# GpSimd splits the row maxima; fp32 exponentials stay in PSUM, with three banks of logits and one of products

## The chip, the core and the metric

The kernel runs on one core of a Trainium2 chip. The metric is device time in microseconds (us) from the start to the end of one execution. Before the change it is 1060.51 us, the median of 3 runs (1059.92 to 1063.94). The engines are TensorE (PE in the profile, with its weight loads as PEld), VectorE (DVE), ScalarE (ACT), GpSimd (POOL) and SyncE (SP), which here only issues DMAs.

## What is computed

A gated cross-attention block followed by a gated feed-forward block with ternary weights, for 8 batches of 224 query rows and 750 context rows of width 512, 16 heads of 32:

```python
q = layer_norm(layernorm(x), gq, betq); c = layer_norm(ctx, gkv, betkv)
Q, K, V = q @ Wq + bq, c @ Wk + bk, c @ Wv + bv          # split into 16 heads
attn = softmax(Q @ K.T * 32**-0.5)                        # 224 x 750 for each head
x = x + tanh(g_xattn) * ((attn @ V) @ Wo + bo)
h = relu(layernorm(x) @ ternary(W1).T + b1)               # 2048 wide
out = x + tanh(g_ffn) * (h @ ternary(W2).T + b2)
```

## The kernel before

Precision comes from pairs of fp16: an operand is kept as a high half and a low half (the fp32 value less the high half), and products of the halves are summed in PSUM.

The work of the batches is a pipeline. `ORDER` lists eleven bodies: OPEN and FIRST (set-up, and the preparation of batch 0), SECOND (attention of batch 0, together with the comparison of the weights that makes them ternary), five INNER bodies, THIRD_LAST, SECOND_LAST and LAST. An INNER body does the attention of one batch, prepares q, k and v of the next (`PREP`), finishes the one before (`FINISH`: normalise, project, feed forward) and normalises the input of the one after the next. Each body has 16 slots, one per head, and `slot_steps` writes the order of the steps in a slot by hand; every engine walks through the same list in order and does its own part of each step. With w0, w1 and w2 for the extra work that `SLOT_WORK` (and `SECOND_WORK`, `SECOND_LAST_WORK`) gives a slot, the order is: score 0, expo 0, w0, expo 1, score 1, w1, expo 2, pv, w2.

- `score` (L437, L776): TensorE makes 128 queries x 750 keys for the head four ahead, in two banks, `ps_score`, which hold one score. VectorE takes the row maximum into `mx` (L779). TensorE's next score waits for that (`max_taken`, L442).
- `split_max` (L782): at the start of every even slot VectorE scales the maxima of two heads by 1/16 and splits them into two fp16 halves, `mhl` (L785, L788). The step `mr` (L518) turns them into rows by four small matmuls, ScalarE copies them into `q_stack`, and the logits of these heads then carry minus the row maximum.
- `expo` (L450, L633, L792): a head has three units of 2 x 125 keys x 224 queries. TensorE writes the logits of a unit into one of two banks, `ps_exp`. ScalarE takes the exponential twice, first in fp32 into `p_full` in SBUF (L642, two buffers), then in fp16 into `ph` (L644). VectorE subtracts: `pl = p_full - ph` (L796). In VectorE's list this stands one unit later than in TensorE's: at expo 0 it does unit 2 of the head before, at expo 1 unit 0, at expo 2 unit 1.
- `pv` (L462): products of `ph` and `pl` with V for the head before, into one of two banks, `ps_pv`; VectorE sums the halves into `o_sum` (`take_o`, L799).
- Fill steps (`q`, `k`, `v`, `f1`, `f2`, ...) go through the two banks of `ps_fill`. For q, k and f1 ScalarE lifts the result to SBUF in fp32, VectorE casts the high half (L871, L876, L892), and GpSimd subtracts for the low half (L1082, L1088, L1092). GpSimd also adds biases to the residual (L1071, L1076), makes the reciprocal deviations by short instructions (L1036 to L1066), and in SECOND the ternary weights (L1101).

The waits that the change touches stand in these lines:

```python
pe.wait_ge(exp_done, b * 48 + (3 * h + u - 1))        # L455, logits: exponential of the unit two back
act.wait_ge(p_split, b * 48 + (k - 1))                # L638, exponentials: subtraction two back (p_full)
pe.wait_ge(o_taken, b * 16 + (h - 1))                 # L468, products: two heads back
```

## Time and profile before

| | |
|---|---|
| median of 3 runs | 1060.51 us (1059.92 to 1063.94) |
| the profiled execution's own time | 1062.24 us |
| its span, first to last instruction | 1060.4 us |
| PE busy | 930.4 us (88%) |
| VectorE busy | 795.4 us (75%) |
| ScalarE busy | 649.6 us (61%) |
| GpSimd busy | 300.6 us (28%) |
| chain that ended last | PE 65%, DVE 20%, ACT 4%, DMA 4%, issue 3%, POOL 2% |
| row maxima, L779 | 256 x 930 ns = 238.2 us on VectorE |
| subtraction of the exponentials, L796 | 384 x 655 ns = 250.7 us on VectorE |
| exponentials, L642 and L644 | 384 x 546 and 384 x 545 ns, 418.9 us on ScalarE |

The busy time of an engine is that of its instructions; matmuls are pipelined, and a busy PE isn't PE at its peak. Successive VectorE instructions overlap a little, so that the time from one start to the next is shorter than the duration. In the waits, "A <- B: total, times, longest" says that A's engine sat idle until B ended. The granted clock of TensorE was 0.952 of full speed over the span. Share of busy time is an average over stages with different limits, so the rows below are read by stretch.

### The profile page before, as it was taken

To read this page: it belongs to the slowest core of one execution; us is meant where nothing else is said; L and a number is where in the kernel's file an instruction comes from. 1 tells how busy PE (TensorE), PEld (TensorE's weight loads), DVE (VectorE), ACT (ScalarE), POOL (GpSimd) and SP (SyncE) were. 2 spreads that over 40 slices of the span, in tenths; PEclk is the share of its full clock that TensorE was granted. 3 is DMA by queue.
4 is the path that set the end of the run, shared out by engine and by line. 5 is a ranking of instruction groups with operands and counts; after the bars stand their busy time and mean duration, and the time that the engine had idled before them with its cause. 6 is when DMAs were issued, how large, how long until landed. Compare 5 with 4: busy or idle time off the path is not lost.

```text
span 1060.4 us, 22598 instructions
## 1 busy us (share of the span) xinstructions
PE 930.4 (88%) x8994; PEld 712.1 (67%) x8994; DVE 795.4 (75%) x1486; ACT 649.6 (61%) x1330; POOL 300.6 (28%) x342
## 2 busy tenths in 40 slices
PE   3777898579989998999989998999899998878868
PEld 0444665466778677876778677876788677757737
DVE  4544799988878889778877788887977777788521
ACT  2755555655777566755775567766775576567511
POOL 4030255333250325123240325032411323033023
PEclk9898798789999999999999999999999999989969
DMA  8495924552202611252222511270223022210000
GB/s 270 140 243 131 203 79 118 138 140 38 56 18 48 172 22 37 59 136 40 58 54 67 115 30 29 60 174 7 52 60 97 1 58 60 62 36 2 19 20 19
DMA packets 56961, 84.03 MB, mean 79 GB/s; under 512 B 6376, under 2 KB 33448, under 8 KB 56856
## 3 DMA queue, kind: packets, MB, share of 16 engines
q1 hardware_dynamic: 50200, 65.80, 25.6%
q10 hardware_dynamic: 6656, 16.78, 5.4%
q8 instruction: 72, 1.18, 0.5%
q14 instruction: 33, 0.27, 0.1%
HBM read 42.20 MB, written 3.67 MB: 43 GB/s over the span
## 4 chain that ended last, share of the span: by engine, by line
PE 65%; DVE 20%; ACT 4%; DMA 4%; issue 3%; POOL 2%; SPq 1%; ACTq 0%; DVEq 0%; POOLq 0%
PE ps_fill L432 43%; PE ps_score L444 7%; PE ps_pv L473 6%; DVE row_max L779 5%; PE ps_exp L457 5%; DVE p_parts L796 4%; PE ps_fill L483 2%; DVE row_max_parts L788 2%; PE ps_fill L525 1%; ACT h_full L692 1%; DVE h_parts L892 1%; DMA ctx_raw<-ctx_in 1%; DVE row_max_parts L785 1%; DMA h_parts<-w1t 1%; DMA x_residual<-x 1%
## 5 line engine op out<-in xcount | busy, mean ns | idle before, releaser
L642 ACT ACTIVATE p_full<-ps_exp 125x448 f32<-125x448 f32 x384 | 209.5, 546 | 161.5 <-PE ps_exp L457 102.0
L796 DVE TENSOR_TENSOR p_parts<-p_full,p_parts 125x448 f16<-125x448 f32 x384 | 250.7, 655 | 2.3 <-ACT p_parts L644 2.3
L779 DVE TENSOR_REDUCE row_max<-ps_score 128x1 f32<-128x750 f32 x256 | 238.2, 930 | 6.6 <-PE ps_score L444 6.6
L644 ACT ACTIVATE p_parts<-ps_exp 125x448 f16<-125x448 f32 x384 | 209.4, 545 | 0.0
L444 PE MATMUL ps_score<-k_stack,q_stack 96*128 96x375 f16 x512 | 131.5, 339 | 72.6 <-DVE row_max L779 56.9
L457 PE MATMUL ps_exp<-q_stack,k_stack 99*125 99x224 f16 x768 | 142.0, 269 | 1.1 <-ACT p_parts L644 0.9
L1092 POOL TENSOR_TENSOR h_parts<-h_full,h_parts 128x448 f16<-128x448 f32 x64 | 79.4, 1241 | 162.9 <-DVE h_parts L892 162.9
L473 PE MATMUL ps_pv<-v_now,p_parts 125*128 125x66 f16 x3072 | 118.6, 196 | 4.0 <-issue 2.7
L457 PEld LDWEIGHTS ps_exp<-q_stack,k_stack 99*125 99x125 f16 x768 | 101.1, 142 | 30.4 <-ACT p_parts L644 2.4
L473 PEld LDWEIGHTS ps_pv<-v_now,p_parts 125*128 125x128 f16 x3072 | 113.5, 99 | 5.9 <-issue 3.3
L432 PE MATMUL ps_fill<-w_ternary,h_parts 128*128 128x256 fp8e4 x1024 | 116.5, 272 | 0.0
L432 PE MATMUL ps_fill<-o_t_hi,w_ternary 128*128 128x224 f16 x512 | 109.1, 269 | 1.3 <-DVE o_t_lo L863 1.3
L444 PEld LDWEIGHTS ps_score<-k_stack,q_stack 96*128 96x128 f16 x512 | 42.7, 99 | 98.4 <-DVE row_max L779 65.1
L432 PE MATMUL ps_fill<-o_t_lo,w_ternary 128*128 128x224 f16 x512 | 108.8, 269 | 0.0
L432 PEld LDWEIGHTS ps_fill<-w_ternary,h_parts 128*128 128x128 f16 x1024 | 99.6, 98 | 11.2
L1088 POOL TENSOR_TENSOR k_stage_lo<-qk_full,k_stage_hi 128x375 f16<-128x375 f32 x64 | 63.1, 989 | 105.2 <-DVE k_stage_hi L876 105.2
L432 PE MATMUL ps_fill<-ctx_t_hi,wk_hi 128*128 128x375 f16 x256 | 82.7, 323 | 3.4 <-ACT qk_full L674 3.4
L432 PE MATMUL ps_fill<-ctx_t_lo,wk_hi 128*128 128x375 f16 x256 | 82.6, 323 | 0.0
L432 PE MATMUL ps_fill<-ctx_t_hi,wk_lo 128*128 128x375 f16 x256 | 82.5, 322 | 0.0
L1082 POOL TENSOR_TENSOR q_stage_lo<-qk_full,q_stage_hi 128x448 f16<-128x448 f32 x16 | 20.6, 1289 | 193.6 <-DVE q_stage_hi L871 193.6
L432 PE MATMUL ps_fill<-wv_hi,ctx_t_hi 128*125 128x512 f16 x192 | 75.4, 393 | 0.0
L432 PE MATMUL ps_fill<-wv_hi,ctx_t_lo 128*125 128x512 f16 x192 | 74.8, 389 | 0.0
(128 smaller groups left out, 1582.4 us busy)
## 6 DMA issues: line engine op xcount, KB each, us to landing
k_stack<-k_stage_hi SPq DMA_DIRECT2D x64, 187.5 KB, 2.7
v_now<-v_stage SPq DMA_DIRECT2D x32, 346.5 KB
ctx_raw<-ctx_in SPq DMA_DIRECT2D x8, 1344.0 KB
h_parts<-w1t ACTq DMA_DIRECT2D x16, 512.0 KB, 4.0
h_parts<-w2t ACTq DMA_DIRECT2D x16, 512.0 KB, 4.1
k_stack<-k_stage_lo SPq DMA_DIRECT2D x32, 187.5 KB, 3.1
x_for_q<-x SPq DMA_DIRECT2D x16, 256.0 KB, 10.2
x_residual<-x SPq DMA_DIRECT2D x16, 256.0 KB, 3.1
```

What stands on the lines that cost most here:

```text
L432: last = pe.matmul(out_ap, left(a, c), right(b_, c), start=(n == 0), stop=(n == chunks * len(order) - 1))
L444: last = pe.matmul(ps_score[:, half, 0:KH], q_stack[0:SPLIT_ROWS, h, QSTART[t]:QSTART[t] + P], k_stack[0:SPLIT_ROWS, h, half * KH:half * K ...
L457: last = pe.matmul(ps_exp[0:KR, (3 * h + u) % 2, (kt % 2) * NQ:(kt % 2) * NQ + NQ], k_stack[0:STACK_ROWS, h, kt * KR:kt * KR + KR], q_stac ...
L473: last = pe.matmul(ps_pv[:, h % 2, t * 2 * VW:(t + 1) * 2 * VW], part[0:KR, 3 * (h % 2) + kt // 2, q0:q0 + P], v_now[0:KR, kt, h].rearrang ...
L483: last = pe.transpose(ps_fill[:, bank, c * size:(c + 1) * size], src[0:rows, c * P:(c + 1) * P], ident[0:rows, 0:rows])
L642: nc.scalar.activation(p_full[0:KR, k % 2, :], ps_exp[0:KR, k % 2, 0:2 * NQ], ACT.Exp, scale=EXP_SCALE)
L644: nc.scalar.activation(ph[0:KR, unit, :], ps_exp[0:KR, k % 2, 0:2 * NQ], ACT.Exp, scale=EXP_SCALE).then_inc(exp_done, 1)
L779: nc.vector.tensor_reduce(mx[:, h, t:t + 1], ps_score[:, :, 0:KH], AX.XY, ALU.max) \
L788: nc.vector.scalar_tensor_tensor(mhl[:, 2 * m:2 * m + 2, :, 1], mx[:, 2 * m:2 * m + 2, :], 1.0 / M_SCALE, mhl[:, 2 * m:2 * m + 2, :, 0], A ...
L796: nc.vector.tensor_tensor(pl[0:KR, unit, :], p_full[0:KR, k % 2, :], ph[0:KR, unit, :], ALU.subtract).then_inc(p_split, 1)
L1088: nc.gpsimd.tensor_tensor(kl[:, i // 2, r], qk_full[:, i % 2, 0:KH], kh[:, i // 2, r], ALU.subtract).then_inc(qk_split, 1)
L1092: nc.gpsimd.tensor_tensor(hl[:, 2 * i:2 * i + 2, :], h_full[:, i % 2, :].rearrange("p (c n) -> p c n", c=2), hh[:, 2 * i:2 * i + 2, :], AL ...
```

## The change

- `split_max` moves from VectorE to GpSimd, at the same places of the order (start of every even slot), as three instructions instead of two: scale `mx` in place, copy to the high half, subtract for the low half, each waiting for the one before. VectorE's first score of a pair of heads waits until the split of the batch before has read `mx`.
- `p_full` is gone. ScalarE makes the fp16 exponential first, then the fp32 one, written over the logits in the same PSUM bank. VectorE subtracts from PSUM.
- `ps_exp` has three banks instead of two, one for each unit of a head. The logits of unit k wait for VectorE's subtraction of unit k-3 (was: ScalarE's exponential of unit k-2), and ScalarE's wait for the subtraction is gone.
- `ps_pv` has one bank instead of two: the products of a head wait until VectorE has taken those of the head before.
- In the set-up, two bias sums use banks of `ps_exp`, and the threshold's matmul waits for `bo_step`, since both now use the one bank of `ps_pv`.

```diff
-        p_full = sb("p_full", [P, 2, 2 * NQ], F32)
-        ps_exp = ctx.enter_context(nc.psum_tensor("ps_exp", [P, 2, 512], F32))
-        ps_pv = ctx.enter_context(nc.psum_tensor("ps_pv", [P, 2, 512], F32))
+        ps_exp = ctx.enter_context(nc.psum_tensor("ps_exp", [P, 3, 512], F32))
+        ps_pv = ctx.enter_context(nc.psum_tensor("ps_pv", [P, 512], F32))
...
-                if not (b * 48 + 3 * h + u < 2):
-                    pe.wait_ge(exp_done, b * 48 + (3 * h + u - 1))
+                if not (b * 48 + 3 * h + u < 3):
+                    pe.wait_ge(p_split, b * 48 + (3 * h + u - 2))
                 for kt in (2 * u, 2 * u + 1):
-                    last = pe.matmul(ps_exp[0:KR, (3 * h + u) % 2, (kt % 2) * NQ:(kt % 2) * NQ + NQ],
+                    last = pe.matmul(ps_exp[0:KR, u, (kt % 2) * NQ:(kt % 2) * NQ + NQ],
...
-                if not (b * 16 + h < 2):
-                    pe.wait_ge(o_taken, b * 16 + (h - 1))
+                if not (b * 16 + h < 1):
+                    pe.wait_ge(o_taken, b * 16 + h)
...
                 pe.wait_ge(tot_ready, 2)
-                pe.matmul(ps_pv[:, 0, 0:2], ones[:, :], abs_tot[:, :], start=True, stop=True).then_inc(tot_all, 1)
+                pe.wait_ge(bo_step, 2)
+                pe.matmul(ps_pv[:, 0:2], ones[:, :], abs_tot[:, :], start=True, stop=True).then_inc(tot_all, 1)
...
                 act.wait_ge(logits_ready, b * 48 + (k + 1))
-                if not (b * 48 + k < 2):
-                    act.wait_ge(p_split, b * 48 + (k - 1))
...
-                nc.scalar.activation(p_full[0:KR, k % 2, :], ps_exp[0:KR, k % 2, 0:2 * NQ], ACT.Exp,
+                nc.scalar.activation(ph[0:KR, unit, :], ps_exp[0:KR, u, 0:2 * NQ], ACT.Exp,
                                      scale=EXP_SCALE)
-                nc.scalar.activation(ph[0:KR, unit, :], ps_exp[0:KR, k % 2, 0:2 * NQ], ACT.Exp,
+                nc.scalar.activation(ps_exp[0:KR, u, 0:2 * NQ], ps_exp[0:KR, u, 0:2 * NQ], ACT.Exp,
                                      scale=EXP_SCALE).then_inc(exp_done, 1)
...
                 dve.wait_ge(scores_ready, n * 32 + (2 * h + t + 1))
+                if t == 0 and h % 2 == 0 and n:
+                    dve.wait_ge(max_split, (n - 1) * 8 + (h // 2 + 1))
...
-                nc.vector.tensor_tensor(pl[0:KR, unit, :], p_full[0:KR, k % 2, :], ph[0:KR, unit, :],
+                nc.vector.tensor_tensor(pl[0:KR, unit, :], ps_exp[0:KR, u, 0:2 * NQ], ph[0:KR, unit, :],
                                         ALU.subtract).then_inc(p_split, 1)
...
+            def split_max(n, m):
+
+                h2 = slice(2 * m, 2 * m + 2)
+                pool.wait_ge(max_taken, n * 32 + (4 * m + 4))
+                nc.gpsimd.tensor_scalar(mx[:, h2, :], mx[:, h2, :], 1.0 / M_SCALE, None, ALU.mult) \
+                    .then_inc(max_scaled, 1)
+                pool.wait_ge(max_scaled, n * 8 + (m + 1))
+                nc.gpsimd.tensor_copy(mhl[:, h2, :, 0], mx[:, h2, :]).then_inc(max_hi, 1)
+                pool.wait_ge(max_hi, n * 8 + (m + 1))
+                nc.gpsimd.tensor_tensor(mhl[:, h2, :, 1], mx[:, h2, :], mhl[:, h2, :, 0],
+                                        ALU.subtract).then_inc(max_split, 1)
```

## Rows read from the trace of the kernel before

**Rows 1.** Stretches: length, busy us of PE, PEld, DVE, ACT, POOL; clock, DMA, GB/s
```profile
112.00:230.00 118.00, 91.65 (x812) 66.85 (x813) 112.23 (x181) 70.05 (x140) 49.73 (x35) 0.85 0.49 123
...
462.00:578.00 116.00, 109.91 (x1120) 86.23 (x1118) 93.50 (x177) 77.02 (x160) 32.65 (x39) 0.99 0.28 67
...
925.00:1010.00 85.00, 69.80 (x842) 57.90 (x840) 65.97 (x124) 55.41 (x119) 19.03 (x20) 0.95 0.10 30
```

**Rows 2.** Waits of PE (us, times, longest) in 112:230, 462:578, 810:925, 925:1010
```profile
PE ps_score L444 <- DVE row_max L779: 17.2, 14, 2.9
...
PE ps_score L444 <- DVE row_max L779: 4.3, 4, 2.5
...
PE ps_score L444 <- DVE row_max L779: 6.1, 7, 1.7
...
PE ps_score L444 <- DVE row_max L779: 9.7, 11, 1.8
```

**Rows 3.** Busy time of L785, L788 and L796 on DVE in 112:230
```profile
112.00:230.00 118.00, 5.51 (x7) 0.85 0.49 123
...
112.00:230.00 118.00, 3.88 (x8) 0.85 0.49 123
...
112.00:230.00 118.00, 34.18 (x47) 0.85 0.49 123
```

**Rows 4.** Groups of the page: busy us, mean ns | idle before, releaser
```profile
L642 ACT ACTIVATE p_full<-ps_exp 125x448 f32<-125x448 f32 x384 | 209.5, 546 | 161.5 <-PE ps_exp L457 102.0 <-DVE p_parts L796 56.2 <-issue 0.2
```

**Rows 5.** Durations of a line: ns min/median/max, first and last start
```profile
L785 DVE TENSOR_SCALAR row_max_parts<-row_max x64: 154/166/1895, 93.1 to 986.7; 128x4 f16<-128x4 f32 x64
...
L788 DVE SCALAR_TENSOR_TENSOR row_max_parts<-row_max,row_max_parts x64: 165/167/2102, 93.3 to 986.9; 128x4 f16<-128x4 f32 x64
...
L796 DVE TENSOR_TENSOR p_parts<-p_full,p_parts x384: 590/616/1929, 114.5 to 1004.5; 125x448 f16<-125x448 f32 x192
...
L854 DVE SCALAR_TENSOR_TENSOR ctx_t_lo<-ps_fill,ctx_t_hi x48: 665/672/683, 28.9 to 807.6; 128x500 f16<-128x500 f32 x48
```

**Rows 6.** DVE in order of time: start, duration; slot 9 of an INNER body
```profile
531.14 0.69 DVE L880 SCALAR_TENSOR_TENSOR v_stage<-ps_fill,v_stage 125x512 f16<-125x512 f32 x1 [0.67 <-ACT v_stage L680]
531.75 0.62 DVE L796 TENSOR_TENSOR p_parts<-p_full,p_parts 125x448 f16<-125x448 f32 x1
532.28 0.93 DVE L779 TENSOR_REDUCE row_max<-ps_score 128x1 f32<-128x750 f32 x1
```

**Rows 7.** DVE in order of time, starts of slots 8 and 10
```profile
522.06 1.02 DVE L788 SCALAR_TENSOR_TENSOR row_max_parts<-row_max,row_max_parts 128x4 f16<-128x4 f32 x1
...
535.23 0.80 DVE L785 TENSOR_SCALAR row_max_parts<-row_max 128x4 f16<-128x4 f32 x1
536.06 1.18 DVE L788 SCALAR_TENSOR_TENSOR row_max_parts<-row_max,row_max_parts 128x4 f16<-128x4 f32 x1
```

**Rows 8.** POOL in order of time, the same places
```profile
522.02 1.03 POOL L1092 TENSOR_TENSOR h_parts<-h_full,h_parts 128x448 f16<-128x448 f32 x1 [2.24 <-DVE h_parts L892]
...
535.96 2.49 POOL L1071 TENSOR_TENSOR x_residual<-x_residual,b_row 128x512 f32<-128x512 f32 x2
```

**Rows 9.** Chain that ended last, in order of time: start, us, what
```profile
523.98 0.49 PE ps_score L444 x2
524.47 0.29 PE ps_fill L525 x4
```

**Rows 10.** DVE in order of time, slot 5 of SECOND_LAST
```profile
948.35 3.23 DVE L796 TENSOR_TENSOR p_parts<-p_full,p_parts 125x448 f16<-125x448 f32 x2
```

**Rows 11.** POOL's groups by shape: busy us, mean ns | idle before
```profile
L1036 POOL TENSOR_TENSOR rstd<-rstd,minus_half 128x8 f32<-128x8 f32 x8 | 13.3, 1664 | 0.7
...
L1042 POOL TENSOR_SCALAR rstd<-rstd 128x2 f32<-128x2 f32 x8 | 3.0, 377 | 0.7
```

**Rows 12.** Busy time by stretch, columns as in rows 1; slots 11 to 13
```profile
542.00:550.00 8.00, 7.98 (x97) 6.45 (x94) 4.56 (x9) 7.21 (x16) 2.23 (x2) 1.00 0.18 46
550.00:558.00 8.00, 7.73 (x87) 6.47 (x86) 6.65 (x14) 7.95 (x17) 0.47 (x1) 1.00 0.65 151
```

More of the change, by code:

```diff
@@ L256, in gated_block @@
         ps_score = ctx.enter_context(nc.psum_tensor("ps_score", [P, 2, 512], F32))
-        ps_exp = ctx.enter_context(nc.psum_tensor("ps_exp", [P, 2, 512], F32))
-        ps_pv = ctx.enter_context(nc.psum_tensor("ps_pv", [P, 2, 512], F32))
+        ps_exp = ctx.enter_context(nc.psum_tensor("ps_exp", [P, 3, 512], F32))
+        ps_pv = ctx.enter_context(nc.psum_tensor("ps_pv", [P, 512], F32))
         ps_fill = ctx.enter_context(nc.psum_tensor("ps_fill", [P, 2, 512], F32))
-        ps_bias = [ps_pv[0:1, 0, :], ps_pv[0:1, 1, :], ps_score[0:1, 0, :]]
+        ps_bias = [ps_exp[0:1, 0, :], ps_exp[0:1, 1, :], ps_score[0:1, 0, :]]
         ctx_loaded, x_loaded, xb_loaded = sem("ctx_loaded"), sem("x_loaded"), sem("xb_loaded")
@@ L281, in gated_block @@
         scores_ready, max_taken = sem("scores_ready"), sem("max_taken")
-        max_hi, max_split = sem("max_hi"), sem("max_split")
+        max_scaled, max_hi, max_split = sem("max_scaled"), sem("max_hi"), sem("max_split")
         shift_rows = sem("shift_rows")
@@ L473, in pv @@
                             last = pe.matmul(
-                                ps_pv[:, h % 2, t * 2 * VW:(t + 1) * 2 * VW],
+                                ps_pv[:, t * 2 * VW:(t + 1) * 2 * VW],
                                 part[0:KR, 3 * (h % 2) + kt // 2, q0:q0 + P],
@@ L575, in bo_sum @@
                 for c in range(DC):
-                    last = pe.matmul(ps_pv[:, 1, :], bv_wide[:, c, :], raw["o"][:, c, :],
+                    last = pe.matmul(ps_pv[:, :], bv_wide[:, c, :], raw["o"][:, c, :],
                                      start=(c == 0), stop=(c == DC - 1))
@@ L977, in body @@
                 for slot in range(H):
-                    m = slot // 2 + 1
-                    if slot % 2 == 0 and (prep if m == H // 2 else attend):
-                        split_max(b if m < H // 2 else b + 1, m % (H // 2))
                     for kind, i in slot_steps(slot, *stages):
@@ L1103, in body @@
             def body(b, stages):
+                attend, prep, finish, norm = stages
                 for slot in range(H):
+                    m = slot // 2 + 1
+                    if slot % 2 == 0 and (prep if m == H // 2 else attend):
+                        split_max(b if m < H // 2 else b + 1, m % (H // 2))
                     for kind, i in slot_steps(slot, *stages):
```

14 lines of the change are left out of this document (3 added, 11 removed).

## Prediction

> **What bounds the kernel now.** I read four views, in this order. The busy time by stretch gives the stages [rows 1]: in the stretch from 112 to 230 us (attention of batch 0, with the weight comparison on VectorE) VectorE works 112.2 of 118 us and TensorE 91.7; in an inner batch, 462 to 578 us, TensorE works 109.9 of 116 and VectorE 93.5; near the end, 925 to 1010 us, TensorE works 69.8 of 85. So VectorE bounds the first stretch, and elsewhere TensorE does, with gaps. The waits of TensorE name the gaps [rows 2]: nearly all are scores that wait for the row maximum of the score before, since ps_score holds one score: 17.2 us in the first stretch, 4.3 in an inner batch, 6.1 and 9.7 in the last two. A change pays only as far as it shortens what VectorE does ahead of such a row maximum. The third view, durations of one line, and the fourth, the order of time on VectorE and GpSimd, show why VectorE is late there.
>
> The two instructions of `split_max` take 166 and 167 ns at the median, but up to 1895 and 2102 [rows 5]. The order of time shows it: the second began at 522.06 and lasted 1.02 us [rows 7] while GpSimd's subtraction of 522.02 ran, 1.03 us [rows 8]; at 535.23 and 536.06 they took 0.80 and 1.18 us [rows 7], the second ending as the first half of GpSimd's 535.96 pair ended (2.49 us for two) [rows 8]. So VectorE stands still on GpSimd's work, and a row maximum stands behind it. `expo`'s subtraction, with both inputs in SBUF, shows the same: median 616 ns, maximum 1929 [rows 5], and two of them took 3.23 us at 948.35 [rows 10]. The subtraction of L854, with one input in PSUM, has 665 to 683 ns over 48 instances [rows 5]: it never stands.
>
> **Part 1: the row maxima are split by GpSimd.** VectorE loses 64 pairs. In the first stretch they cost 5.51 + 3.88 = 9.4 us [rows 3]; in an inner batch two pairs stand before a waiting score: 1.1 us at slot 8 (0.2 us for the first instruction, estimated from its median and the step to the next, and 1.02, less overlap [rows 5, 7]) and 0.80 + 1.18 = 2.0 at slot 10 [rows 7].
>
> GpSimd gains three small instructions per pair of heads. Its own small ones bound the price: 377 ns mean for a 128x2 multiply, 1664 for the 128x8 power [rows 11]. I take 0.3 us each, 0.9 in all, nearest to the multiply (the power is another operation): some 58 us over the kernel, on an engine that is mostly idle [rows 1]. Ends for the range: 0.6 and 4 us. What is queued behind them: the low halves of q, k and f1, which come later in the slot and wait for VectorE anyway, and the residual's bias, which waits for its DMA. What they queue behind: the last low half of the slot before. Who waits: the `mr` matmuls. Tightest is mr 5, in slot 8. There GpSimd's subtraction ends at 522.02 + 1.03 = 523.05 [rows 8], the split then at about 523.95; without the pair the row maximum ends 1.1 us earlier, so the score of 523.98 starts at 522.9, and mr 5, at 524.47 before [rows 9], asks at 523.4 and gets its rows at 523.95. So slot 8 gives 0.5 us and not 1.1. The other `mr` steps have work of 2 us and more ahead of them.
>
> **Part 2: the fp32 exponentials go to PSUM.** 384 subtractions now read one input from PSUM. I price one by the row that has such an input: L880, 512 columns, began at 531.14 and let the next start 0.61 us later; the SBUF subtraction of 448 columns at 531.75 let the next start after 0.53 [rows 6]. The 64 columns between them make 0.07 (from L796's 0.53 us for 448), so the place of the input costs about nothing; ends: 0.06 us less or more for each. What goes is the standing: 34.2 us for 47 in the first stretch [rows 3] against 47 x 0.616 = 29.0 [rows 5], so 5.2 us there, and 1.3 at the pair of 948.35 (3.23 less two medians is 2.0, of which I count what a score waits for) [rows 10].
>
> The rows above show no dearer PSUM input. The Trainium skill ("Perfetto Trace Analysis", Optimizing Scalar/DVE Operations) states about 60 ns of access overhead for DVE on SBUF and about 125 on PSUM; by it each of the 384 would cost 65 ns more, 25 us of VectorE in all, an estimate from that page. What that would do to the end is the second rival.
>
> ScalarE's second exponential now reads and writes the same PSUM bank. No row shows ScalarE writing PSUM. By the SBUF form, 546 ns mean [rows 4], I take the same; ends: 0.05 us less, and twice the streaming, 0.4 us more. ScalarE also loses its wait for p_full's two buffers, 56.2 us [rows 4], to a wait inside TensorE.
>
> **Part 3: three banks of logits, one of products.** TensorE's logits of unit k wait for the subtraction of unit k-3 where they waited for the exponential of unit k-2. VectorE does the first unit of the head before ahead of its second row maximum, which TensorE's next score has already waited for; the third follows its row maximum directly, and the products need it anyway; the second stands behind one VectorE step, with a fill of TensorE between. The single bank of products needs `take_o` of the head before, which VectorE does before the row maximum that the second score of the slot waits for. All are therefore older than a wait that TensorE has passed: cost 0, cover the score waits. Only in the last four slots of SECOND_LAST, which have no scores, is that cover gone; there the work between is long, and I allow 0 to 0.5 us a slot. The set-up's moved banks and its added wait come long after their data: 0.
>
> **The sum**, against the profiled execution (1062.2 us, span 1060.4):
> first stretch: 9.4 + 5.2 = 14.6 us off VectorE. Not all comes back, since TensorE waits 17.2 us there only in pieces and work elsewhere is then late; counting at each waiting score no more than its wait, I get 8.
> Inner batches, five: slot 8 gives 0.5, slot 10 gives 2.0 (the next thing late there is the cast that stood beside GpSimd just before, which the change leaves), and two small waits later in the batch, within the 4.3 [rows 2], 0.3: 2.8 x 5 = 14.
> Batch before the last: 0.5, 1.7 and 0.7: 3 of its 6.1. Last attention: 1.3 from the pair at 948.35, 1.0 each at slots 8 and 10, and 0.3 at two pairs without standing: 4 of its 9.7.
> 8 + 14 + 3 + 4 = 29. 1062.2 - 29 = 1033.2; the median lies 1.7 below the profiled execution: 1031.5, said as **1032**.
>
> **Rivals.** *Time that returns.* VectorE's casts still share with GpSimd, which now works more often (cast L892 beside it, and the casts of k and q), and a removed gap opens at the next late thing. If half the gain returns: 1062.2 - 14.5 - 1.7 = 1046. For it: the first stretch is dense on both engines. Against: in an inner batch the row maximum follows directly on the pair. 0.15.
>
> *A dearer PSUM input.* At 0.06 us more, from the end above, the first stretch loses 47 x 0.06 = 2.8 us and each later batch some 10 subtractions in VectorE's late stretches, 0.6 us, by 7 batches 4: 1032 + 7 = 1039. The step of L880 speaks against it. The page's 65 ns, named above, is this rival's rule. 0.15.
>
> *ScalarE's write in place at double streaming.* Then ScalarE, busy 7.21 + 7.95 of 16 us from 542 to 558 [rows 12], where it also normalises, becomes the bound there: seven units at 0.4 us are 2.8 us, less 0.8 of idle, 2.0 in each of 7 batches, 14: 1046. 0.08.
>
> *The other side: GpSimd late for `mr`.* If each small instruction took 1.3 us, on the way to the power's 1.66 [rows 11], the split took some 4 us. Then mr 5 comes 2.6 us later than before, the `mr` of slots 12 and 14, which have 2 to 3 us of cover, 1.4 and 0.8: 4.8 us a batch against the 3.2 a batch gained elsewhere. It decides from about 3.4 us per split. 1062.2 + 8 x 1.6 - 1.7 = 1073. Against it: the multiply's 377 ns. 0.06.
>
> *More than counted.* Each VectorE advance is kept through the following slots, and most of the score waits go: of the 37 us in the four stretches shown, with the four other inner batches some 54, 42 come back: 1062.2 - 42 - 1.7 = 1018. 0.12.
>
> **How the numbers follow.** My forecast has 0.44; with the rivals that makes 1. Leaving out the rival at 1073 and part of those at either end, the range is 1018 to 1049, which also holds the bounds of parts 2 and 3. About 0.5% (5 us) is what a measurement of this kernel tells from no change: faster 0.86, within 0.08 (the tails of the two rivals at 1046), slower 0.06.
>
> **What would show it.** Right: L796's maximum falls from 1929 ns to near its median; the pair is gone from VectorE; TensorE's wait for the row maximum in an inner batch falls from 4.3 us to below 2; a wait of about 0.5 us for GpSimd before mr 5. Wrong: a median of L796 above 680 ns; a second exponential much over 546; three splits on GpSimd that take over 2 us together, with `mr` waiting; casts on VectorE that take the standing over.

## The result, and the profile after

The changed kernel takes 1015.72 us (median of 4 runs, 1011.18 to 1018.24); the kernel before takes 1060.22 in the same measurement. The ratio is 0.958, 95% interval 0.953 to 0.963. I had forecast 1032 us, between 1018 and 1049: the direction is right, the gain of 44.5 us is half as large again as the 29 I had summed, and the median lies just below the range. The profiled execution is the one of 1018.24 us, with a span of 1016.4. Of the kernel before, two executions beside the experiments (1227.76 and 4825.26 us) were in a slow state and count in no median or ratio here.

The page of the kernel after: its busy times with their shares of the span, and the groups that answer to [rows 4]; columns are line, engine, operation, out<-in, count | busy us, mean ns | idle before it, released by.

```profile
PE 917.1 (90%) x8994; PEld 704.0 (69%) x8994; DVE 735.9 (72%) x1358; ACT 643.5 (63%) x1330; POOL 307.8 (30%) x534
...
L640 ACT ACTIVATE p_parts<-ps_exp 125x448 f16<-125x448 f32 x384 | 209.0, 544 | 112.9 <-PE ps_exp L456 110.9
...
L786 DVE TENSOR_TENSOR p_parts<-ps_exp,p_parts 125x448 f16<-125x448 f32 x384 | 235.5, 615 | 2.5 <-ACT ps_exp L642 2.5
L642 ACT ACTIVATE ps_exp<-ps_exp 125x448 f32<-125x448 f32 x384 | 210.8, 549 | 0.0
```

The exponential in place in PSUM takes 549 ns, where the one into SBUF took 546 [rows 4], and ScalarE no longer waits for VectorE.

The stretches that answer to [rows 1], with the same columns: the first stretch, an inner batch, and the last attention.

```profile
110.00:218.00 108.00, 87.40 (x806) 62.62 (x805) 98.18 (x166) 68.50 (x139) 49.54 (x55) 0.90 0.50 127
441.50:552.00 110.50, 107.85 (x1122) 85.79 (x1121) 85.91 (x162) 76.35 (x160) 33.10 (x63) 1.00 0.30 71
882.00:956.00 74.00, 64.00 (x791) 51.87 (x790) 59.11 (x109) 55.23 (x120) 19.55 (x39) 1.00 0.13 35
```

An inner batch is now bounded by TensorE almost alone, 107.85 of 110.5 us. TensorE's waits (us in total, times, longest), over the whole span and then in the inner batch from 441.5 to 552:

```profile
PE ps_score L443 <- DVE row_max L779: 27.3, 33, 2.6
...
PE ps_fill L524 <- POOL row_max_parts L1092: 8.3, 7, 3.1
...
PE ps_score L443 <- DVE ctx_t_lo L844: 1.4, 1, 1.4
PE ps_fill L524 <- POOL row_max_parts L1092: 0.9, 1, 0.9
```

In the inner batch no score waits for a row maximum any more, where 4.3 us went [rows 2]; one new wait, of 0.9 us, is for GpSimd's split. The durations that answer to [rows 5] (ns, minimum/median/maximum), and the line that now has the low halves of h on GpSimd, which was L1092 before:

```profile
L786 DVE TENSOR_TENSOR p_parts<-ps_exp,p_parts x384: 590/615/627, 111.3 to 960.9; 125x448 f16<-125x448 f32 x192
...
L1079 POOL TENSOR_TENSOR h_parts<-h_full,h_parts x64: 1032/1035/1043, 275.5 to 1000.0; 128x448 f16<-128x448 f32 x64
```

The same line of the kernel before, for comparison:

```profile
L1092 POOL TENSOR_TENSOR h_parts<-h_full,h_parts x64: 1032/1346/1358, 286.7 to 1044.0; 128x448 f16<-128x448 f32 x64
```

The subtraction's median has not moved (616 ns before [rows 5]), but its maximum fell from 1929 ns to 627. And GpSimd's subtraction, which the change doesn't touch, went from a median of 1346 ns to 1035. That median overstates it, since it also moves with when GpSimd comes to the line (see the run e6_sbuf_full); the mean fell from 1241 to 1036 ns, the maximum from 1358 to 1043. The standing went both ways, and at these two lines it is gone.

**Where the 44 us came from.** I cut each profiled execution at the start of ScalarE's first exponential of each batch (in the kernel before, 462.00 us for an inner one). "Inner" is the five bodies from 228.9 us on in the kernel before; "last attention" ends at the first exponential of its last head. A slot goes here from the first exponential of its head to that of the next head.

```
us                        set-up  1st stretch  inner x5  batch before last  last attention  rest
before                     113.5     115.4       580.2        110.9             79.2        61.3
after                      110.3     107.3       556.1        108.4             73.8        60.6
gain                         3.2       8.1        24.1          2.5              5.4         0.7
forecast                     0         8          14            3                4           0
```

The first stretch and the two parts behind the inner batches are as summed, within 1.4 us. The inner batches gave 24 us where I had 14. Most of it lies at one place, slot 10: it became shorter by 3.84, 4.08, 4.05, 2.43 and 3.99 us in the five batches, where I had put 2.0 each.

**A second cost in the same gap.** In the kernel before, TensorE pauses 2.46 us at slot 10 ahead of the second score of the slot. What its own clock does behind that pause I hadn't looked at. Busy time by stretch for 4 us just behind the pause, in the five inner batches of the kernel before; the third number from the end is the granted clock:

```profile
306.00:310.00 4.00, 3.55 (x23) 2.81 (x24) 2.91 (x5) 1.04 (x3) 2.09 (x2) 0.57 0.00 0
422.00:426.00 4.00, 4.00 (x34) 3.25 (x33) 2.35 (x4) 1.40 (x4) 1.52 (x2) 0.57 0.00 0
538.00:542.00 4.00, 3.85 (x26) 3.02 (x27) 2.61 (x5) 1.14 (x3) 1.79 (x2) 0.57 0.02 4
654.00:658.00 4.00, 3.11 (x48) 2.88 (x48) 3.58 (x6) 2.02 (x5) 2.54 (x2) 1.00 0.01 4
770.00:774.00 4.00, 4.00 (x43) 3.37 (x41) 2.60 (x6) 3.15 (x7) 2.39 (x2) 0.57 0.02 4
```

And TensorE in order of time just behind it, in two of these batches (start, duration; in brackets the idle time before):

```profile
538.15 0.81 PE L444 MATMUL ps_score<-k_stack,q_stack 96*128 96x375 f16 x2 [2.46 <-DVE row_max L779]
538.75 0.39 PE L432 MATMUL ps_fill<-o_t_hi,w_ternary 128*128 128x224 f16 x1
...
654.89 0.49 PE L444 MATMUL ps_score<-k_stack,q_stack 96*128 96x375 f16 x2 [2.46 <-DVE row_max L779]
655.23 0.26 PE L432 MATMUL ps_fill<-o_t_hi,w_ternary 128*128 128x224 f16 x1
```

In four of the five batches the pause is followed by half clock (1.2 GHz of 2.4), and a matmul takes 0.39 us instead of 0.26; in the batch of 654.89 the clock stays. A mean of 0.57 over 4 us is 3.4 us at half clock and the rest at full clock, so that a fall can cost 1.7 us at most. That batch is also the one that gained 2.43 us where the others gained some 4.0. So a fall costs about 1.6 us, and the change takes four away. In the kernel after, the same place has full clock:

```profile
513.50:517.50 4.00, 3.94 (x53) 3.34 (x52) 2.65 (x6) 4.00 (x12) 3.44 (x7) 1.00 0.01 4
```

### The profile page after: what moved, and what is told of

The parts are those of the page before. It is cut to its first block, busy times and chain, and to the rows that moved or that the text cites. A ratio compares the mean times of both kernels' runs of the same rounds, so it can differ in the third digit from the quotient of the medians.

```text
span 1016.4 us, 22463 instructions
## 1 busy us (share of the span) xinstructions
PE 917.1 (90%) x8994; PEld 704.0 (69%) x8994; DVE 735.9 (72%) x1358; ACT 643.5 (63%) x1330; POOL 307.8 (30%) x534
## 3 DMA queue, kind: packets, MB, share of 16 engines
q8 instruction: 72, 1.18, 0.5%
## 4 chain that ended last, share of the span: by engine, by line
PE 62%; DVE 8%; ACT 5%; POOL 2%; issue 1%; DMA 1%; SPq 1%; ACTq 0%
PE ps_fill L431 42%; PE ps_score L443 6%; PE ps_pv L472 5%; PE ps_exp L456 5%; DVE row_max L779 2%; PE ps_fill L482 2%; DVE p_parts L786 2%; ACT h_full L690 2%; PE ps_fill L524 1%; ACT ps_exp L642 1%; ACT ctx_raw L700 1%; POOL h_parts L1079 1%; DVE h_parts L882 1%; DMA x_residual<-x 1%; DVE rows_to_turn L804 1%
## 5 line engine op out<-in xcount | busy, mean ns | idle before, releaser
L779 DVE TENSOR_REDUCE row_max<-ps_score 128x1 f32<-128x750 f32 x256 | 237.9, 929 | 12.4 <-PE ps_score L443 10.1
L786 DVE TENSOR_TENSOR p_parts<-ps_exp,p_parts 125x448 f16<-125x448 f32 x384 | 235.5, 615 | 2.5 <-ACT ps_exp L642 2.5
L642 ACT ACTIVATE ps_exp<-ps_exp 125x448 f32<-125x448 f32 x384 | 210.8, 549 | 0.0
L443 PE MATMUL ps_score<-k_stack,q_stack 96*128 96x375 f16 x512 | 128.2, 332 | 43.1 <-DVE row_max L779 27.3
L456 PEld LDWEIGHTS ps_exp<-q_stack,k_stack 99*125 99x125 f16 x768 | 98.1, 140 | 35.4 <-DVE p_parts L786 9.0
L472 PE MATMUL ps_pv<-v_now,p_parts 125*128 125x66 f16 x3072 | 115.8, 194 | 1.1 <-DVE p_parts L786 1.1
L431 PE MATMUL ps_fill<-o_t_hi,w_ternary 128*128 128x224 f16 x512 | 104.4, 262 | 1.3 <-DVE o_t_lo L853 1.3
L1079 POOL TENSOR_TENSOR h_parts<-h_full,h_parts 128x448 f16<-128x448 f32 x64 | 66.3, 1036 | 129.1 <-DVE h_parts L882 129.0
L431 PE MATMUL ps_fill<-o_t_lo,w_ternary 128*128 128x224 f16 x512 | 104.2, 262 | 0.0
L1075 POOL TENSOR_TENSOR k_stage_lo<-qk_full,k_stage_hi 128x375 f16<-128x375 f32 x64 | 56.2, 882 | 97.0 <-DVE k_stage_hi L866 97.0
L431 PE MATMUL ps_fill<-wv_lo,ctx_t_hi 128*125 128x512 f16 x192 | 74.2, 386 | 0.0
```

What stands on the lines that cost most here:

```text
L431: last = pe.matmul(out_ap, left(a, c), right(b_, c), start=(n == 0), stop=(n == chunks * len(order) - 1))
L443: last = pe.matmul(ps_score[:, half, 0:KH], q_stack[0:SPLIT_ROWS, h, QSTART[t]:QSTART[t] + P], k_stack[0:SPLIT_ROWS, h, half * KH:half * K ...
L456: last = pe.matmul(ps_exp[0:KR, u, (kt % 2) * NQ:(kt % 2) * NQ + NQ], k_stack[0:STACK_ROWS, h, kt * KR:kt * KR + KR], q_stack[0:STACK_ROWS ...
L472: last = pe.matmul(ps_pv[:, t * 2 * VW:(t + 1) * 2 * VW], part[0:KR, 3 * (h % 2) + kt // 2, q0:q0 + P], v_now[0:KR, kt, h].rearrange("p a ...
L642: nc.scalar.activation(ps_exp[0:KR, u, 0:2 * NQ], ps_exp[0:KR, u, 0:2 * NQ], ACT.Exp, scale=EXP_SCALE).then_inc(exp_done, 1)
L779: nc.vector.tensor_reduce(mx[:, h, t:t + 1], ps_score[:, :, 0:KH], AX.XY, ALU.max) \
```

## The experiments

Runs of one group share one chip and one measurement of the kernel before (1058.36, 1057.82 and 1058.31 us for the three groups: first e1 to e4, then e5, e6, d6 and after_again, then e7, d4 and before_again). I first asked whether each part alone brings its share, with the theory that the excess is the clock (and the pause behind it), against the rival that it is the banks.

**The split alone (e1_split_only).** Part 1 as in the diff, applied to the kernel before; exponentials and banks stay.

```diff
-                nc.vector.tensor_scalar(mhl[:, 2 * m:2 * m + 2, :, 0], mx[:, 2 * m:2 * m + 2, :], 1.0 / M_SCALE,
-                                        None, ALU.mult).then_inc(max_hi, 1)
...
+                nc.gpsimd.tensor_scalar(mx[:, h2, :], mx[:, h2, :], 1.0 / M_SCALE, None, ALU.mult) \
+                    .then_inc(max_scaled, 1)
...
```

> Part 1 alone: the kernel before with the row maxima split by GpSimd; p_full in SBUF, two banks of logits and two of products stay. The theory of the clock says that the 15 us beyond the forecast come from slot 10 of the inner batches: the pair of split instructions left TensorE idle for 2.46 us there, and the granted clock then stood at half for 3.4 us in four of five inner batches, 1.7 us lost each time. The pair is gone here too, so most of the 44 us comes: about 1025 us (1020 to 1030), no half-clock stretch between 230 and 920 us; what is missing is the standing of L796. The theory of the banks (the third bank of logits carries the surplus) says 1034 us or more.

1041.29 us, ratio 0.983 (0.979 to 0.987), 17 us gained: less than the theory of the clock gave it, and a time that the rival had named too (1034 us or more). This run alone doesn't decide between them; the run with three banks and the operand in SBUF does, below. The inner batches give 12.4 us. Slot 10 shortens by 2.90, 3.12, 3.10, 1.47 and 3.03 us; again the batch whose clock had not fallen gives 1.6 less, and the clock doesn't fall to half at slot 10 of any inner batch here. The whole pause of 2.46 us ahead of the score is gone, with part 1 alone, but a new wait has come. GpSimd at slot 10, in order of time:

```profile
521.44 1.35 POOL L1081 TENSOR_TENSOR h_parts<-h_full,h_parts 128x448 f16<-128x448 f32 x1 [0.33 <-DVE h_parts L884]
522.75 2.88 POOL L1060 TENSOR_TENSOR x_residual<-x_residual,b_row 128x512 f32<-128x512 f32 x2
525.72 0.25 POOL L1089 TENSOR_SCALAR row_max<-row_max 128x4 f32<-128x4 f32 x1
...
526.55 0.20 POOL L1094 TENSOR_TENSOR row_max_parts<-row_max,row_max_parts 128x4 f16<-128x4 f32 x1
```

The split stands behind the residual's additions, which take 2.88 us, 0.38 more than in the changed kernel, and TensorE waits 0.96 us for it in each inner batch. (At slot 8 it waits 1.40 us for the split there, 0.86 in the changed kernel.) The account of the slot is 2.46 (the pause) + 1.6 (the clock) - 0.96 = 3.1. Over the whole kernel this wait has grown well over the 8.3 us of the changed one:

```profile
PE ps_fill L525 <- POOL row_max_parts L1094: 20.0, 16, 3.9
```

**Parts 2 and 3 alone (e2_psum_only).** The split stays on VectorE.

```diff
-                nc.scalar.activation(p_full[0:KR, k % 2, :], ps_exp[0:KR, k % 2, 0:2 * NQ], ACT.Exp,
+                nc.scalar.activation(ps_exp[0:KR, u, 0:2 * NQ], ps_exp[0:KR, u, 0:2 * NQ], ACT.Exp,
```

> Parts 2 and 3 alone: exponentials written over the logits in PSUM, three banks of logits, one of products; VectorE still splits the row maxima. The theory of the clock says 8 to 12 us come (1049 to 1053 us): the subtractions no longer stand, the splits still do, and the clock still falls at slot 10. The theory of the banks says 20 us or more (1040 us or less).

1035.39 us, ratio 0.980 (0.974 to 0.987): more than the clock theory had for it, and in the rival's range, though not for the rival's reason: the run e6_sbuf_full shows that the third bank isn't what gains. Slot 10 gives 2.15, 2.38, 2.35, 0.71 and 2.28 us. Its order of time on VectorE and TensorE there:

```profile
519.81 0.82 DVE L890 CAST h_parts<-h_full 128x448 f16<-128x448 f32 x1 [0.17 <-ACT h_full L690]
...
521.29 0.49 DVE L783 TENSOR_SCALAR row_max_parts<-row_max 128x4 f16<-128x4 f32 x1
521.81 1.18 DVE L786 SCALAR_TENSOR_TENSOR row_max_parts<-row_max,row_max_parts 128x4 f16<-128x4 f32 x1
...
523.90 0.50 PE L443 MATMUL ps_score<-k_stack,q_stack 96*128 96x375 f16 x2 [1.77 <-DVE row_max L777]
```

The pair is still there, its second instruction still 1.18 us, but the pause has fallen from 2.46 to 1.77, since the cast and the first instruction now stand less (0.82 and 0.49 us, against 1.19 and the 0.80 of [rows 7]), and after a pause of 1.77 us the clock stays in all five batches. The shorter pause gives 0.7 of each slot's 2.3 us; the clock the other 1.6.

**Two banks (e3_two_banks).** The changed kernel, with the logits of unit k in bank k % 2.

```diff
-                    pe.wait_ge(p_split, b * 48 + (3 * h + u - 2))
+                    pe.wait_ge(p_split, b * 48 + (3 * h + u - 1))
...
-                    last = pe.matmul(ps_exp[0:KR, u, (kt % 2) * NQ:(kt % 2) * NQ + NQ],
+                    last = pe.matmul(ps_exp[0:KR, (3 * h + u) % 2, (kt % 2) * NQ:(kt % 2) * NQ + NQ],
```

> The changed kernel with two banks of logits in use instead of three, so that the logits of unit k wait for VectorE's subtraction of unit k-2. The theory of the clock says that this wait is covered by the waits of the scores except where VectorE is late: 0 to 3 us slower than the changed kernel, 1016 to 1019 us. The theory of the banks says at least 8 us slower, 1024 us or more.

1121.04 us, ratio 1.059 (1.053 to 1.064): 105 us slower than the changed kernel's 1015.72. The wait that appears:

```profile
PE ps_exp L456 <- DVE p_parts L786: 100.5, 132, 2.7
```

The rival's number came here, and by far more than it said: with the exponential in PSUM, a bank is held until VectorE's subtraction, and with two banks TensorE waits for it 132 times. But this doesn't say that a third bank brings anything to the kernel before; it is the price of the place, as the run e6_sbuf_full shows.

**Only slot 10's pair (e4_slot10_only).** The kernel before, with only the pair of maxima of slot 10 split by GpSimd.

```diff
-                    if slot % 2 == 0 and (prep if m == H // 2 else attend):
+                    if slot % 2 == 0 and m != 6 and (prep if m == H // 2 else attend):
```

> The kernel before with one of the eight splits of a batch, that at slot 10 (heads 12 and 13), moved to GpSimd. My forecast's price of that place, 2.0 us a batch, gives 12 us over the batches: 1048 us. The theory of the clock gives 1.7 us more in each of the four batches where the clock fell: 4 us each there, 2.4 in the others, 19 us: about 1041 us, and no half-clock stretch in the inner batches.

1044.17 us, ratio 0.987 (0.982 to 0.992): between the two expectations. No half clock behind slot 10 in any inner batch. Slot 10 gives 2.34, 2.57, 2.54, 0.91 and 2.48 us. In order of time there, VectorE and TensorE:

```profile
524.88 1.19 DVE L898 CAST h_parts<-h_full 128x448 f16<-128x448 f32 x1 [0.17 <-ACT h_full L694]
...
527.71 0.49 PE L446 MATMUL ps_score<-k_stack,q_stack 96*128 96x375 f16 x2 [0.52 <-DVE row_max L783]
531.62 0.36 PE L527 MATMUL ps_fill<-ident,row_max_parts 128*2 128x128 f16 x4 [0.96 <-POOL row_max_parts L1111]
```

The pause falls from 2.46 to 0.52 us, so the pair was worth 1.94, as forecast (2.0); the 0.52 that remain go with the cast, which still takes 1.19 us beside GpSimd: it did in each inner batch of this run, and where the cast is shorter (0.63 us with the whole split moved), nothing remains. The fall of the clock gives 1.6, and the split's wait of 0.96 takes some back: 1.94 + 1.6 - 0.96 = 2.6. Without the clock the slot would have gained 1.0, as it nearly did (0.91) in the batch without a fall.

**Which part of the PSUM parts (e6_sbuf_full).** The changed kernel with the fp32 exponential in two SBUF buffers again, and three banks of logits. The logits then wait for ScalarE's exponential of unit k-3, not for VectorE's subtraction, so TensorE's wait is the looser one.

```diff
-                    pe.wait_ge(p_split, b * 48 + (3 * h + u - 2))
+                    pe.wait_ge(exp_done, b * 48 + (3 * h + u - 2))
...
-                nc.scalar.activation(ps_exp[0:KR, u, 0:2 * NQ], ps_exp[0:KR, u, 0:2 * NQ], ACT.Exp,
+                if not (b * 48 + k < 2):
+                    act.wait_ge(p_split, b * 48 + (k - 1))
+                nc.scalar.activation(p_full[0:KR, k % 2, :], ps_exp[0:KR, u, 0:2 * NQ], ACT.Exp,
```

> Whole change, except that the fp32 exponential goes to two buffers in SBUF again, with ScalarE's wait for the subtraction of two units before; three banks of logits and one bank for the products with V stay. It takes the third bank apart from the place of the operand. Theory A, what the parts with PSUM gain comes from the subtraction no longer reading both operands from SBUF, so that GpSimd and VectorE stand less behind each other: the cast and GpSimd's low halves take their old times again, and the time is that of the kernel with only the split moved, 1038 to 1043 us. Rival B, the gain is the third bank and ScalarE's freedom: within 4 us of the changed kernel, 1015 to 1020 us.

1042.60 us, ratio 0.986 (0.983 to 0.988), 27.9 us slower than the changed kernel on the same chip (1014.74) and level with the split alone. Its groups:

```profile
L789 DVE TENSOR_TENSOR p_parts<-p_full,p_parts 125x448 f16<-125x448 f32 x384 | 262.4, 685 | 2.5 <-ACT p_full L645 2.4
...
L1082 POOL TENSOR_TENSOR h_parts<-h_full,h_parts 128x448 f16<-128x448 f32 x64 | 75.0, 1172 | 120.8 <-DVE h_parts L885 120.8
```

And one of its waits of TensorE:

```profile
PE ps_fill L525 <- POOL row_max_parts L1095: 18.0, 14, 3.7
```

The third bank by itself brings nothing, though TensorE's wait for a bank is looser here. What returns is the standing: 685 ns mean for the subtraction against 615, with a maximum of 1922 against 627; for GpSimd's low half a mean of 1172 against 1036 and a maximum of 1354 against 1043. Its median stays at 1037 here, as it does with the split alone (1035): the fall of the median from 1346 is not the operand's. The waits for the split are 18.0 us against 8.3; in each inner batch 1.40 us at slot 8 and 0.96 at slot 10, as with the split alone.

**ScalarE's wait (e7_act_waits).** The last run differed from the changed kernel also by a wait on ScalarE, the only wait that it had more; here only that one is put back.

```diff
+                if not (b * 48 + k < 2):
+                    act.wait_ge(p_split, b * 48 + (k - 1))
                 nc.scalar.activation(ps_exp[0:KR, u, 0:2 * NQ], ps_exp[0:KR, u, 0:2 * NQ], ACT.Exp,
```

> Whole change, with ScalarE's wait for the subtraction of two units before put back ahead of the fp32 exponential; this stays in PSUM, in three banks. The run with two buffers in SBUF was 28 us slower than the changed kernel and differed from it in the place of the operand and in this wait. Theory A, the place makes all of it: within 4 us of the changed kernel, 1013 to 1019 us, with GpSimd's low halves at 1.04 us as there. Rival B, the wait does: 1035 to 1043 us.

1017.11 us, ratio 0.962 (0.957 to 0.967): the changed kernel's time. Its inner batches have 556.1 us, as there. The wait is worth nothing, and the place of the operand makes the 28 us.

**The pause by itself (d6, d4).** The changed kernel, with extra reductions on VectorE at slot 10 of the inner batches, six and four.

```diff
+                    if stages == INNER and slot == 10:
+                        for e in range(6):
+                            nc.vector.tensor_reduce(spare[:, 8 * (b - 1) + e:8 * (b - 1) + e + 1],
+                                                    whl["o"][0][:, e % 4, :], AX.X, ALU.max)
```

> Whole change, with six more reductions of about 0.6 us on VectorE at the start of slot 10 of each of the five inner batches, so that TensorE again finds a pause there, of 2.5 to 3.5 us by the 3.6 us added. Theory A, a pause of about 2.5 us is what brought half the granted clock for the next 3.4 us in the kernel before: the clock falls again behind the pause, and a batch becomes longer by the pause and another 1.6 us, 4 to 5 us in all, 1036 to 1041 us. Rival B, the fall came from something else of the kernel before: no half clock in the inner batches, and 2.5 to 3.5 us a batch, 1028 to 1033 us.

> Whole change, with four extra reductions on VectorE at the start of slot 10 of the five inner batches, where the run with six made a pause of 3.27 us and brought half clock behind it in four of them, +4.8 us each, and +3.2 us in the fifth. The pause should be 3.27 less two reductions of 0.6, so 2.0 to 2.1 us, between the 1.77 us of the kernel with only the PSUM parts, where the clock stayed, and the 2.46 us of the kernel before, where it fell. Theory A, a pause of this length still leaves the clock alone: +2.0 us a batch, 1025 us. Rival B, it brings it down: +3.6 us a batch in four, 1031 us.

Six: 1038.33 us. Four: 1031.46 us, one execution each, so that their profiles carry the argument. With six, TensorE pauses 3.27 us in all five batches; against the changed kernel, slot 10 grows by 4.83, 4.73, 3.21, 4.85 and 4.83 us, and the granted clock is half behind the pause in all but the third. With four, the pause is 2.08 to 2.21 us, and the slot grows by 2.02, 2.03, 3.59, 2.14 and 2.02; here only the third has half clock. The two batches of 4 us behind the pause (six reductions, third and fourth batch, then four reductions, third and fourth):

```profile
525.00:529.00 4.00, 3.67 (x51) 3.23 (x52) 3.27 (x7) 1.60 (x5) 1.35 (x2) 1.00 0.02 4
639.50:643.50 4.00, 3.97 (x29) 3.37 (x30) 2.18 (x4) 0.59 (x2) 1.03 (x1) 0.57 0.02 4
...
519.50:523.50 4.00, 3.95 (x41) 3.59 (x42) 2.65 (x6) 1.62 (x5) 1.40 (x3) 0.66 0.01 4
634.00:638.00 4.00, 3.88 (x52) 3.36 (x53) 3.27 (x8) 2.11 (x6) 1.94 (x4) 1.00 0.02 4
```

A slot's growth is the pause, within 0.1 us, and 1.5 to 1.6 us more where the clock falls, and only there. That a pause at this place brings the fall, and what the fall costs, is shown: it went with the pause, came back with it, and came more often with the longer one. For d4 neither expectation is whole: one fall of five, and 1031 us where the inner batches explain 12.6 us and the rest is set-up and the last part.

**The kernel before again (before_again).**

> The kernel before once more. It is asked two things. Its set-up: theory, the 3.1 us between the starts of the first exponentials of the two profiles are chance, so this one starts anywhere from 107 to 114 us. Its clock: theory, the fall to half clock behind slot 10 is this kernel's own, so it is there again in three to five of the five inner batches, each of which is 115 to 116 us long; rival, the falls were chance of that one execution, so none or one here and inner batches of 113.5 to 114 us.

1059.55 us, ratio 1.001 (0.998 to 1.004). The clock is half behind the pause of slot 10 in all five inner batches here; the batches have 115.6 to 118.1 us, four of them above the 115 to 116 expected (115.1 to 117.5 in the first profile). The slot that had kept its clock in the first profile is 1.61 us longer, and every other slot 10 within 0.2. So the 24 us of the inner batches hold four falls in the profile shown, and would hold five with this one. The first exponential starts at 113.4 us, within the expectation.

**Both kernels' set-up, and a try for more (after_again, e5_early_split).** The last takes GpSimd's split one slot earlier:

```diff
+                        if early and kind == "score" and i == 1:
+                            split_max(b if m < H // 2 else b + 1, m % (H // 2))
+                            early = False
```

> The changed kernel once more, on one chip with the three kernels beside it. All theories: 1011 to 1020 us. The set-up ends between 108 and 113 us on every chip so far whatever the kernel, so that its end, 110.3 us in the changed kernel's profile and 113.5 us in the one of before, is taken for chance; if this profile has it outside 110 +/- 3, that is wrong.

> Whole change, with GpSimd's split of a pair of maxima issued one slot earlier, straight behind the unit that turns the pair's last score, so ahead of the low halves of W1 and W2 in the queue. In the changed kernel TensorE waits 0.86 us for the split of slot 8 in each of six batches and 3.1 us in the first (8.3 us in all). Theory A, GpSimd's order in its queue makes these waits: they go, and the time falls by 5 to 8 us, to about 1008 us. Rival B, VectorE's maxima are themselves that late, or the wait only moves to the fills that now stand behind the split: within 2 us of the changed kernel.

1014.74 us and 1014.89 us: level. The set-up of the changed kernel ends at 108.7 us this time, inside the 110 +/- 3. In the early one the wait for the split is gone, but

```profile
PE ps_score L443 <- DVE row_max L779: 31.8, 41, 2.6
```

has grown from 27.3. Slot 8 became 0.93 us shorter in every inner batch and slots 10 and 11 took 0.57 of it back. VectorE and GpSimd in order of time just ahead of slot 10, in the changed kernel and in the early one, and the score there in the early one:

```profile
510.34 1.04 POOL L1079 TENSOR_TENSOR h_parts<-h_full,h_parts 128x448 f16<-128x448 f32 x1
...
511.26 0.39 DVE L882 CAST h_parts<-h_full 128x448 f16<-128x448 f32 x1 [0.17 <-ACT h_full L690]
...
509.41 1.03 POOL L1079 TENSOR_TENSOR h_parts<-h_full,h_parts 128x448 f16<-128x448 f32 x1
...
509.49 1.21 DVE L882 CAST h_parts<-h_full 128x448 f16<-128x448 f32 x1 [0.17 <-ACT h_full L690]
...
512.33 0.49 PE L443 MATMUL ps_score<-k_stack,q_stack 96*128 96x375 f16 x2 [0.53 <-DVE row_max L779]
```

In both the cast ends some 0.25 us behind the low half on GpSimd. Without the wait at slot 8 it begins at the low half's start and takes 1.21 us, as in the kernel before, and the pause of 0.53 us is back at slot 10, with the fp32 exponential in PSUM. The rival was right, and the cast is the reason. 0.4 us a batch stays, less than these runs can tell apart, and I have no version that beats the changed kernel.

## Why the prediction was right, and where it was wrong

**Part 1, right in its price, right at its place.** VectorE loses the pair: 1.94 us at slot 10 (2.0 forecast). GpSimd's three instructions take 228, 191 and 232 ns in the mean, where I had taken 300 each; with the steps between them the split at slot 8 takes 0.92 us from its first start to its end, where I had 0.9. Slot 8 in order of time, GpSimd:

```profile
500.10 1.03 POOL L1079 TENSOR_TENSOR h_parts<-h_full,h_parts 128x448 f16<-128x448 f32 x1 [2.54 <-DVE h_parts L882]
501.22 0.22 POOL L1087 TENSOR_SCALAR row_max<-row_max 128x4 f32<-128x4 f32 x1
501.51 0.19 POOL L1090 CAST row_max_parts<-row_max 128x4 f16<-128x4 f32 x1
501.79 0.35 POOL L1092 TENSOR_TENSOR row_max_parts<-row_max,row_max_parts 128x4 f16<-128x4 f32 x1
```

The split ends 1.0 us after the low half that it queues behind, as foreseen, and TensorE waits for it: 0.86 us, not 0.5, so the slot gave 0.2 and not 0.5. That "the other `mr` steps have work of 2 us and more ahead of them" was too easy, though: at slot 10 the changed kernel has 0.14 us to spare,

```profile
515.93 0.21 POOL L1092 TENSOR_TENSOR row_max_parts<-row_max,row_max_parts 128x4 f16<-128x4 f32 x1
...
516.28 0.36 PE L524 MATMUL ps_fill<-ident,row_max_parts 128*2 128x128 f16 x4
```

(516.28 less 515.93 + 0.21), and without part 2 it waits 0.96 us. Of what GpSimd queues ahead of that split, the residual's additions, I had said only that they wait for their DMA.

**Part 2, right that its price is nothing, too small in what it frees.** A PSUM operand costs the subtraction nothing: 615 ns against 616. The Trainium skill ("Perfetto Trace Analysis", Optimizing Scalar/DVE Operations) gives about 60 ns of access overhead for VectorE on SBUF and about 125 on PSUM; no row of this subtraction shows the 65 ns between them. ScalarE read PSUM before and after, so that its 549 against 546 ns say only that the place of its output costs nothing. But I counted the standing only where the subtraction itself stood. The other half is on GpSimd: with the operand in SBUF (e6_sbuf_full) its low halves take 1172 ns in the mean and the split comes later, 18.0 us of TensorE's waits for it against 8.3. The Trainium skill ("SBUF — State Buffer", SBUF: two separate sides) describes just this: an exclusive lock that either side may hold for a whole instruction, among others against a VectorE operation with two inputs in SBUF. The traces agree: with the operand in SBUF and in PSUM, the subtraction's maximum is 1922 and 627 ns (e6_sbuf_full and the changed kernel), that of GpSimd's low half 1354 and 1043.

**The step that failed** is the term "slot 10 gives 2.0 (the next thing late there is the cast that stood beside GpSimd just before, which the change leaves)". The pair itself was priced right, 1.94 us. What the term had at nothing is the clock: a pause of TensorE was priced at its length, and it cost its length and 1.6 us of half clock behind it. Slot 10 gave 18.4 us over the five batches where I had 10. Of this 12.3 are the pause, 5 x 2.46, and the other 6.1 the four falls of the clock. The clock was to be seen in the trace of before; I had read the granted clock only as a mean over a batch, 0.99 [rows 1], in which 3.4 us at half clock out of 116 hardly show.

The smaller part of the error is that the change doesn't leave the cast: 2.46 us of pause go and not 2.0. It isn't part 2 that does it, since the split alone takes the whole pause away. At this place of the kernel before GpSimd and VectorE ran like this:

```profile
533.28 1.04 POOL L1092 TENSOR_TENSOR h_parts<-h_full,h_parts 128x448 f16<-128x448 f32 x1
...
533.38 1.19 DVE L892 CAST h_parts<-h_full 128x448 f16<-128x448 f32 x1 [0.17 <-ACT h_full L692]
```

The cast ends 0.25 to 0.29 us behind the low half in every run, and is the shorter the later it begins beside it: 1.19 us in the kernel before and with only slot 10's pair moved, 0.82 with the PSUM parts alone, 0.63 with the split alone, 0.39 in the changed kernel. In the changed kernel TensorE comes to it late, having waited 0.86 us for the split at slot 8; the early split takes that wait away and has the 1.21 us and a pause of 0.53 back. So these 0.5 us of slot 10 were in the main paid at slot 8. There I had 0.5 a batch and got 0.2. That makes 8.4 us more at slot 10, 1.5 less at slot 8, and 3.2 more in small waits elsewhere than the 1.5 forecast: 10 us. The largest of the small ones, 0.17 to 1.33 us a batch, is at slot 1. It comes with part 2: the PSUM parts alone give 0.17 to 1.32 us there, the split alone -0.58 to 0.34.

**The first stretch** came out as summed, 8.1 for 8, but its parts don't add: the split alone gives 2.4 us there, the PSUM parts 3.4, both together 8.1. Alone, the split is late on a GpSimd that still stands (6.0 us of TensorE's waits for it there, 3.1 in the changed kernel), which is part of the difference. The clock goes with the rest: over this stretch its granted mean was 0.85 and 0.84 in the two profiles of the kernel before, 0.86 with the split alone, 0.84 with the PSUM parts alone, 0.83 with the operand back in SBUF, and 0.90 in both profiles of the changed kernel. VectorE bounds much of this stretch, so how much of the time the clock makes isn't shown. The sum had no such term; that 8 was right is in part luck.

**The last attention** gave 5.4 us for 4. The clock is in it too. The kernels with extra reductions are the changed kernel there; their last attention took 75.3 and 75.2 us at a mean clock of 0.95, against 73.8 and 73.7 at full clock in the two profiles of the changed kernel. The kernel before had half clock there for 6.8 us in both profiles. So some 1.5 of the 5.4 us are the clock's, and without it the 4 was about right.

**Part 3**: three banks cost next to nothing, as forecast: TensorE waits 2.3 us in all for the subtraction, where it waited 0.9 us for the exponential before. With two banks the kernel is 105 us slower, and 80 us slower than the split alone. One bank of products shows no wait for the one before.

**The set-up** I had at 0 and it gave 3.2 us in the two profiles. Two profiles of the kernel before have 113.5 and 113.4 us, the two of the changed kernel 110.3 and 108.7, and the kernel with only slot 10's pair moved, whose set-up is the old one, 108.0. Among these TensorE waits between 16.6 and 18.5 us for its first DMA, and the granted clock from 60 to 113 us differs too. Over all thirteen profiles it ends at 108.0 to 113.5 us with the old set-up (four) and at 107.8 to 112.1 us with the new one (nine). So I count the 3.2 us as chance and not as the change's, though with so few profiles a smaller difference can't be ruled out.

**The rivals.** "More than counted", 1018 us at 0.12, was the one that came nearest, for a reason that it doesn't name. "Time that returns" and the late `mr` appear in small: 0.96 us at slot 10 of the kernels without part 2, 0.86 us at slot 8 of the changed one, 0.57 of the 0.93 us of the early split. The dearer PSUM input and ScalarE's double streaming didn't come.

## What to carry to other kernels

Before pricing the removal of a pause of TensorE, read the granted clock right behind it, in stretches of a few microseconds: a mean over a batch hides it. Where GpSimd and VectorE both work from SBUF, a VectorE operation with two SBUF inputs slowed both engines here; count what moving it frees on each, and on whatever queues behind. How long an instruction stands depends on when it begins beside the other engine's, so a wait removed at one place can come back at the next. And if an operand moves to PSUM, count who holds the bank until when; here the kernel with one bank fewer was 105 us slower.

## What the runs showed of the hardware

- The three small GpSimd instructions of 128x4 took 0.19 to 0.35 us at slot 8; with the wait of each for the one before, they started 0.29 and 0.28 us apart.
- At slot 10 of the inner batches half clock (1.2 GHz) followed on TensorE's pauses of 2.46 us in nine of ten cases (two profiles of the kernel before), of 3.27 us in four of five, of 2.1 to 2.2 us in one of five, and of 1.77 us in none of five. Each fall made the slot 1.5 to 1.6 us longer.
- The length of one pause doesn't decide alone. In the last attention, where TensorE works less (64.0 us of 74, against 107.85 of 110.5 in an inner batch), the clock fell behind a pause of 1.80 us (943.49 us in the second profile of the kernel before). With six extra reductions it fell there, 6.3 us behind the start of that part, without a pause over 1.2 us ahead of it; in the changed kernel it stayed at the same place. TensorE had been busy for 3.86 of the 6.3 us in both, so what decides in the single case I don't know. The 3.4 us that follow, first with six reductions and then in the changed kernel, with the same columns as the stretches above:

```profile
909.70:913.10 3.40, 3.40 (x35) 3.04 (x34) 3.36 (x7) 1.78 (x4) 0.61 (x3) 0.50 0.44 120
...
888.40:891.80 3.40, 2.75 (x39) 2.14 (x38) 3.40 (x8) 2.24 (x6) 0.62 (x3) 1.00 0.33 98
```

- VectorE's cast of 128x448, 0.39 us at the median, took 0.39 to 1.22 us just ahead of slot 10, by when it began beside GpSimd's subtraction of 1.04 us; it ended 0.25 to 0.29 us behind that.
- ScalarE took the same time to read and write one PSUM bank in place as to read PSUM and write SBUF: 549 ns and 546 ns for 125x448.
